# Seven half-size products in place of eight for the gate and up products of an FFN, on one Trainium2 core

## The reference, cut to what matters

```
h = layernorm(x)                       # 2048 x 512
W = scale * (4-bit weight - zero)      # 512 x (2 x 1376), unpacked on the chip
hidden = silu(h @ W_gate) * (h @ W_up) # 2048 x 1376
x = x + hidden @ W_down                # 1376 x 512
```

## Time and profile before

| | |
|---|---|
| median of 3 executions | 2420.39 us (2418.84 to 2422.48) |
| the profiled execution's own time | 2423.2 us |
| its span, first to last instruction | 2421.4 us |
| TensorE busy | 2368.5 us, 98% |
| granted TensorE clock, mean | 0.993 |
| FFN steps (1, 1) to (4, 3) | 1078.8 to 1321.5 us of the span |

### The profile page before, as it was taken

The page is one execution under the profiler, slowest core; times in us unless marked ns, Lnnn a source line. Parts: engine busy times, 40 slices in busy tenths (PEclk is TensorE's granted clock), DMA queues, the critical chain, the costliest instruction groups (busy, mean ns, idle before and its releaser), DMA issues.

```text
span 2421.4 us, 45108 instructions
## 1 busy us (share of the span) xinstructions
PE 2368.5 (98%) x17660; PEld 1297.3 (54%) x17668; DVE 1624.8 (67%) x3133; ACT 1252.7 (52%) x2423; POOL 1226.8 (51%) x983
## 2 busy tenths in 40 slices
PE   8899999999999999999999989999999999999998
PEld 4555555555555555444444655555555555555554
DVE  8877777777777798754444666667666666656566
ACT  7666565655555555333232554555555555544453
POOL 4556666666666666233232445445555555445531
PEclk9999999999999999999999999999999999999999
DMA  6111121212121111011100011122121212221101
GB/s 211 45 45 36 45 53 27 54 27 53 32 55 30 42 40 28 27 44 36 44 11 30 27 31 28 44 53 62 36 62 36 62 36 62 53 43 27 27 14 70
DMA packets 216753, 108.13 MB, mean 45 GB/s; under 512 B 169280, under 2 KB 192480, under 8 KB 216544
## 3 DMA queue, kind: packets, MB, share of 16 engines
q1 hardware_dynamic: 216544, 105.25, 17.6%
HBM read 61.62 MB, written 4.19 MB: 27 GB/s over the span
## 4 chain that ended last, share of the span: by engine, by line
PE 63%; POOL 14%; DVE 12%; ACT 5%; issue 5%; DMA 0%; POOLq 0%; SPq 0%; DVEq 0%; ACTq 0%
PE PB L867 17%; PE PB L819 15%; PE PB L979 9%; PE PB L803 6%; POOL AR L2720 5%; PE PB L996 5%; POOL AR L2725 4%; POOL PSP L2738 3%; DVE WB L1938 2%; DVE AR L2136 2%; PE PB L844 2%; PE PB L909 2%; PE PB L775 1%; POOL AR L2715 1%; ACT JUNK L1332 1%
## 5 line engine op out<-in xcount | busy, mean ns | idle before, releaser
L867 PE MATMUL PB<-WB,AR 128*128 128x512 f16 x3072 | 685.5, 380 | 1.5 <-DVE AR L2136 1.1
L819 PE MATMUL PB<-XTB,WB 128*128 128x512 f16 x3072 | 682.3, 381 | 2.6 <-DVE WB L1938 1.5
L867 PEld LDWEIGHTS PB<-WB,AR 128*128 128x128 f16 x3072 | 298.5, 98 | 356.7 <-issue 8.5
L819 PEld LDWEIGHTS PB<-XTB,WB 128*128 128x128 f16 x3072 | 298.3, 98 | 348.7 <-issue 10.3
L2731 POOL TENSOR_TENSOR AR<-AR,SML 128x512 f32<-128x512 f32 x128 | 144.7, 1152 | 317.1 <-DVE SML L2121 317.1
L2151 DVE SCALAR_TENSOR_TENSOR X<-PB,SML,X 128x512 f32<-128x512 f32 x256 | 189.3, 747 | 169.4 <-PE PB L867 163.4
L1492 ACT ACTIVATE AR<-PB 128x512 f16<-128x512 f32 x256 | 131.4, 595 | 232.6 <-PE PB L909 232.4
L2031 DVE TENSOR_TENSOR AR<-PB,AR 128x512 f16<-128x512 f32 x128 | 88.2, 691 | 168.0 <-ACT AR L1455 168.0
L2720 POOL TENSOR_TENSOR AR<-AR,CST 128x512 f32<-128x512 f32 x128 | 183.0, 1430 | 31.3 <-ACT AR L1402 31.3
L979 PE MATMUL PB<-XTB,AR 128*128 128x512 f16 (+1 forms) x864 | 192.5, 379 | 0.0
L1408 ACT ACTIVATE AR<-AR 128x512 f16<-128x512 f32 x128 | 80.5, 630 | 196.1 <-POOL AR L2725 194.7
(11 more groups left out here) (273 smaller groups left out, 3775.7 us busy)
## 6 DMA issues: line engine op xcount, KB each, us to landing
STG<-in_wo SPq DMA_DIRECT2D x14, 1024.0 KB
STG<-in_wq SPq DMA_DIRECT2D x13, 1024.0 KB
STG<-in_qw_gu SPq DMA_DIRECT2D x40, 128.0 KB
STG<-in_ctxT SPq DMA_DIRECT2D x4, 1024.0 KB
X<-in_x SPq DMA_DIRECT2D x4, 1024.0 KB, 10.8
out_x<-X SPq DMA_DIRECT2D x16, 256.0 KB, 2.4
STG<-in_wk SPq DMA_DIRECT2D x14, 256.0 KB
STG<-in_wv SPq DMA_DIRECT2D x14, 256.0 KB
```

What stands on the lines that cost most here:

```text
L819: m = pe.do.matmul(b[:, :], wq[x][:, k, h * 128:(h + 1) * 128], XT[y][c][:, k, :], start=n == 0, stop=n == 11)
L867: m = pe.do.matmul(b[:, :], AT[x][:, h, t * 128:(t + 1) * 128], wo[y][:, h, :], start=n == 0, stop=n == 11)
```

## The change

It applies to blocks s = 2, 3, 4, all chunks: twelve steps, called folded. W's block and x's chunk are seen as 2 by 2 blocks: K in two halves of 256, hidden columns in two tiles of 128 (gate and up side by side), tokens in two sets of 256. Eight block products become seven (P1 to P7), each two outputs (gate, up) of 2 slices of K x 3 = 6 matmuls 256 wide: 84 matmuls. P5, P6 and P7 multiply two sums of blocks, P3 and P4 one sum and one block, P1 and P2 two blocks.

- The sums of W (4 per block, `fold_w`, 512 columns each) are made on GpSimd, in the staging area, their halves on ScalarE and GpSimd (`fold_w_halves`). The staging area is free for the next load only after that.
- The sums of x (per chunk 4 `join_x` and 4 `fold_x` on GpSimd; 4 `fold_x_halves`, each one ScalarE copy and one VectorE subtraction; 512 columns each). They go where the context halves `CTB` lie, which the second layer needs: so `CTB` (4 x 1 MB) is written to DRAM after unit 12 of the first attention, and read back behind step (4, c).
- P1 is copied out of PSUM by ScalarE, VectorE adds the others to buffers in SBUF (`CB`): 7 additions per step. Silu, hidden values and their halves then work in 4 pieces of 256 tokens rather than 2 of 512.
- In the planner: unpacking of block 2 moves to (1,0) side 3, (1,1) sides 0, 1 and 3; the down weights of block s + 1, s from 1 to 4, to (s,3) sides 0 and 2 (only side 0 for s = 4). The places of `unpack` during blocks 2 to 4 stay.

```diff
+            def product(s, c, name, b, wt, xs):
+                for g in range(2):
+                    n = 0
+                    o = b[:, 256 * g:256 * g + 256].rearrange("p (a n) -> p a n", a=2)
+                    for k in range(2):
+                        for x, y in THREE:
+                            m = pe.do.matmul(o, wt[x][:, k, g, :], xs[y][:, k, :, :], start=n == 0, stop=n == 5)
+                            n += 1
+                m.then_inc(gu_mm.of((s, c, name)), 1)
...
+                product(s, c, "P1", bank(0, (p_out, (s, c, "P1"))), a11, b11)
...
+                product(s, c, "P6", bank(1, (p_sum, (s, c, "P1+P6"))), sw[1], sx[1])
+                product(s, c, "P5", bank(2, (p_sum, (s, c, "P1+P6+P5")), (p_sum, (s, c, 1, 1))), sw[0], sx[0])
+                product(s, c, "P2", bank(3, (p_sum, (s, c, 0, 0))), a12, b21)
...
+                product(s, c, "P7", bank(1, (p_sum, (s, c, "P1+P6+P7"))), sw[2], sx[2])
+                product(s, c, "P3", bank(0, (p_sum, (s, c, 0, 1))), sw[3], b22)
+                product(s, c, "P4", bank(3, (p_sum, (s, c, 1, 0))), a22, sx[3])
...
                 side("f", s, c, 0)
-                gate_up(s, c, 0)
+                if folded(s, c):
+                    folded_first(s, c)
+                else:
+                    gate_up(s, c, 0)
                 side("f", s, c, 1)
                 down(*FFN[i - 1], (0, 1))
                 side("f", s, c, 2)
-                if s < 5:
+                if folded(s, c):
+                    folded_last(s, c)
+                elif s < 5:
                     gate_up(s, c, 1)
                 down(*FFN[i - 1], (2, 3))
                 side("f", s, c, 3)
```

ScalarE's order in a folded step:

```diff
+                    product_out(s, c, "P1", 0, (0, 0))
+                    folded_gate(s, c, 0, 0)
+                    folded_hidden(s, c, 0, 0)
+                    side("f", s, c, 1)
+                    side("f", s, c, 2)
+                    folded_gate(s, c, 1, 1)
+                    folded_gate(s, c, 0, 1)
+                    folded_hidden(s, c, 1, 1)
+                    folded_gate(s, c, 1, 0)
+                    folded_hidden(s, c, 0, 1)
+                    folded_hidden(s, c, 1, 0)
+                    side("f", s, c, 3)
```

VectorE's part, in the places where `hidden` stood, and the sums of x:

```diff
+            def fold_x_halves(c, i):
+                dve.wait_ge(xs_hi, (c, i))
+                dve.do.tensor_tensor(SUMX[1][c][i], XF[i], SUMX[0][c][i], ALU.subtract).then_inc(xs_lo.of((c, i)), 1)
+
+            def product_add(s, c, key, name, bank, dst, src):
+                dve.wait_ge(gu_mm, (s, c, name))
+                dve.do.tensor_tensor(CB[BLOCK[dst]], PB[bank][:, :], CB[BLOCK[src]], ALU.add).then_inc(p_sum.of((s, c, *key)), 1)
...
+            def folded_first(s, c):
+                dve.wait_ge(p_out, (s, c, "P1"))
+                product_add(s, c, ("P1+P6",), "P6", 1, (1, 0), (0, 0))
+                dve.wait_ge(p_sum, (s, c, "P1+P6"))
+                product_add(s, c, ("P1+P6+P5",), "P5", 2, (0, 1), (1, 0))
+                product_add(s, c, (0, 0), "P2", 3, (0, 0), (0, 0))
+                folded_hidden(s, c, 0, 0)
+
+            def folded_last(s, c):
+                product_add(s, c, ("P1+P6+P7",), "P7", 1, (1, 0), (1, 0))
+                dve.wait_ge(p_sum, (s, c, "P1+P6+P7"))
+                product_add(s, c, (1, 1), "P5", 2, (1, 1), (1, 0))
+                product_add(s, c, (0, 1), "P3", 0, (0, 1), (0, 1))
+                folded_hidden(s, c, 1, 1)
+                product_add(s, c, (1, 0), "P4", 3, (1, 0), (1, 0))
+                folded_hidden(s, c, 0, 1)
+                folded_hidden(s, c, 1, 0)
```

The planner and SyncE:

```diff
-                where = (((2, 3), (3, 0), (3, 1), (3, 2)), ((0, 3), (1, 1), (1, 3), (2, 1)))[s][k] if s < 2 else \
+                where = (((2, 3), (3, 0), (3, 1), (3, 2)), ((0, 3), (1, 0), (1, 1), (1, 3)))[s][k] if s < 2 else \
                     (k // 2, 1 + 2 * (k % 2))
...
-                plan_f(*(((0, 3, 3), (1, 0, 1))[j] if s == 0 else (s, 2, 2 + j if s == 1 else 1 + 2 * j)), "unpack_d", s + 1, j)
+                plan_f(*(((0, 3, 3), (1, 0, 1))[j] if s == 0 else (s, 3, 2 * j)), "unpack_d", s + 1, j)
+
+        for step, places in ((2, ((1, 2, 0), (1, 2, 1), (1, 2, 2), (1, 2, 3))), (3, ((2, 2, 0), (2, 2, 1), (2, 2, 2), (2, 2, 3))),
+                             (4, ((3, 2, 0), (3, 2, 1), (3, 2, 2), (3, 2, 3)))):
+            for n, where in enumerate(places):
+                for i in ((0, 2), (1, 3))[n % 2]:
+                    plan_f(*where, "fold_w_halves" if n > 1 else "fold_w", step, i)
+        for c, places in ((0, ((0, 2, 1), (0, 2, 2), (0, 2, 3), (0, 3, 0), (0, 3, 1), (0, 3, 2))),
+                          (1, ((0, 3, 3), (1, 0, 0), (1, 0, 1), (1, 0, 2), (1, 0, 3), (1, 1, 0))),
+                          (2, ((1, 3, 0), (1, 3, 1), (1, 3, 2), (1, 3, 3), (2, 0, 0), (2, 0, 1))),
+                          (3, ((2, 0, 2), (2, 0, 3), (2, 1, 0), (2, 1, 1), (2, 1, 2), (2, 1, 3)))):
+            for n, where in enumerate(places):
+                for i in ((0, 1), (2, 3), (0, 2), (1, 3), (0, 1), (2, 3))[n]:
+                    plan_f(*where, ("join_x", "fold_x", "fold_x_halves")[n // 2], c, i)
...
-                return [(uq_lo, (key[1], KT - 1))]
+                return [(ws_lo, (key[1], 3)) if 2 <= key[1] <= 4 else (uq_lo, (key[1], KT - 1))]
...
+                sp.do.dma_start(kept[:, 4096 * c:4096 * c + 4096], CTB[:, 4096 * c:4096 * c + 4096]
...
+                    if (L, u) == (0, 12):
+                        keep_contexts()
```

More of the change, by code:

```diff
@@ L94, in build @@
         every = []
+        kept = nc.dram_tensor("kept", (128, 4096 * NC), F16, kind="Internal").ap()
         def signal(name):
@@ new lines, in folded_last @@
+            def folded_last(s, c):
+                pl = place(s)
+                a22 = [w_part(GUW[pl][n], 1, 1) for n in range(2)]
+                b22 = [x_part(n, c, 1, 1) for n in range(2)]
+                sw = [[SUMW[pl][n][i].rearrange("p (k g n) -> p k g n", k=2, g=2) for n in range(2)] for i in range(4)]
+                sx = [[by_kan(SUMX[n][c][i]) for n in range(2)] for i in range(4)]
+                product(s, c, "P7", bank(1, (p_sum, (s, c, "P1+P6+P7"))), sw[2], sx[2])
+                product(s, c, "P3", bank(0, (p_sum, (s, c, 0, 1))), sw[3], b22)
+                product(s, c, "P4", bank(3, (p_sum, (s, c, 1, 0))), a22, sx[3])
@@ L1355, in high @@
                     act.wait_ge(y_mm, (0, 3, 3))
+                    if kind == 2:
+                        act.wait_ge(xs_lo, (3, 3))
                 elif (L, g) == (1, 1):
@@ L1558, in gated @@
                 if i > 0 and j < len(step_tiles(FFN[i - 1][0])):
-                    act.wait_ge(h_lo, (*FFN[i - 1], j))
+                    for key in h_keys(*FFN[i - 1], j):
+                        act.wait_ge(h_lo, key)
                 if i == 0:
@@ L1576, in hidden, with fold_w_halves, product_out, folded_gate @@
                 act.do.activation(HB[(4 * s + c) % 2][0][0:wd, j, :], SG[j][0:wd, :], copy).then_inc(h_hi.of((s, c, j)), 1)
+            def fold_w_halves(s, i):
+                j, ki = SUM_AT[i]
+                act.wait_ge(wf, (s, i))
+                act.do.activation(SUMW[place(s)][0][i].rearrange("p (k g n) -> p k g n", k=2, g=2),
+                                  w_part(AREA[0].rearrange("p (k f) -> p k f", k=4), ki, j), copy).then_inc(ws_hi.of((s, i)), 1)
+            def fold_x_halves(c, i):
+                act.wait_ge(ct_kept[c], c)
+                act.wait_ge(v_mm, (0, UNIT[0][NKV - 1, c], 0))
+                act.wait_ge(xf, (c, i))
+                act.do.activation(SUMX[0][c][i], XF[i], copy).then_inc(xs_hi.of((c, i)), 1)
+            def product_out(s, c, name, bank, block):
+                before_it = FFN[FFN.index((s, c)) - 1]
+                act.wait_ge(gu_mm, (s, c, name))
+                if folded(*before_it):
+                    act.wait_ge(hf, (*before_it, *block))
+                act.do.activation(CB[BLOCK[block]], PB[bank][:, :], copy).then_inc(p_out.of((s, c, name)), 1)
+            def folded_gate(s, c, j, t):
+                act.wait_ge(p_sum, (s, c, j, t))
+                for key in h_keys(*FFN[FFN.index((s, c)) - 1], j):
+                    if len(key) == 3 or key[3] == t:
+                        act.wait_ge(h_lo, key)
+                act.do.activation(sg_part(j, t), CB[BLOCK[j, t]][:, 0:256], ACTF.Silu, scale=power(("sc", 0))).then_inc(silu_ok.of((s, c, j, t)), 1)
+            def folded_hidden(s, c, j, t):
+                i = FFN.index((s, c))
+                act.wait_ge(hf, (s, c, j, t))
+                act.wait_ge(y_mm, (*FFN[i - 2], 3))
+                act.do.activation(hb_part(s, c, 0, j, t), sg_part(j, t).rearrange("p (a n) -> p a n", a=2), copy
+                                  ).then_inc(h_hi.of((s, c, j, t)), 1)
             def tail_setup(part):
@@ L2655, in vector @@
                 side("f", s, c, 0)
-                hidden(s, c, 0)
+                if folded(s, c):
+                    folded_first(s, c)
+                else:
+                    hidden(s, c, 0)
```

(9 more changed lines are left out.)

124 lines of the change are left out of this document (113 added, 11 removed).

## The result

The changed kernel takes 2427.76 us (median of 8 runs, 2425.11 to 2430.93) against 2421.01 for the kernel before (8 runs, 2418.84 to 2422.54): ratio 1.003, 95% interval 1.002 to 1.0039, 6.75 us more. The forecast was 2417.5. The profiled execution took 2428.07, its span is 2425.1.

What follows compares the result with a forecast made beforehand. TensorE was taken to bound the FFN. Products -14.4, waits +2.4, +7.1, +0.5 and +1.5 sum to -2.9 us: profiled execution 2420.3, median 2417.5 us, range 2409 to 2428.

Steps and rivals of the forecast that it cites:

- The products: Folded steps on TensorE: 84 matmuls at 0.109 us, 9.17 instead of 10.37 us a step, 14.4 us less in twelve.
- Wait 1: (1,1) side 0: TensorE waits 2.4 us, uncovered, for VectorE's multiply from bank 5, shared by two adjacent unpackings.
- Wait 2: (2,0) to (2,2): VectorE, late with x sums and unpacking, frees banks late; 3.8 + 0.2 + 1.6 + 1.5, 7.1 us.
- Wait 3: (3,3) into (4,0): ScalarE's 5.0 us scaling delays the silus, so the down product waits 0.5 us for a hidden half.
- Wait 4: (4,3) side 2: the late load of w(1,1,1) delays ScalarE's squares, so the `peak` matmul waits 1.5 us.
- The DMA's zero: Context write after unit 12 and reads back in (4,1) to (5,0): taken to cost 0 us.
- B: Rival: VectorE bounds every step with unpacking, its instructions stretched beside GpSimd; +7 us, 2427.5; chance 0.25.
- A: Rival: waits mostly absorbed, lateness in (1,3) and (2,0) partly parallel; -10 us, 2410.4; chance 0.28.
- C: Rival: products miss the 0.109 us pace, at 0.13 a step's take 10.9 us; +14 us, 2434; chance 0.05.

Runs made afterwards that it cites:

- unpacking_moved_only: The kernel before with only the unpacking of slices 1, 2 and 3 in block 1 moved to (1,1) sides 0, 1 and 3; ratio 1.0008.
- contexts_only: The kernel before with only the write of the context halves to DRAM and the reads back; 2420.41 us, ratio 0.9999.
- last_sums_later: The changed kernel with the four halvings of chunk 3's x sums moved from (2,1) sides 2 and 3 to (2,2) sides 0 and 1; 2428.33 us.

## Why the prediction was wrong

The products were right: 1.31 us per product, 1.20 per step (block 3 is 4.8 us shorter, four steps), 14.4 in all. By the prediction's estimate from the section Back-to-back issue gap of TensorE: Matmul & The Clock Gate in the Trainium skill the new kernel was to lose 23 us here; the trace disagrees, at 256 wide as at 512 (0.109 and 0.216 us a matmul).

What failed is the step that sized and listed the waits, 11.5 us on record, 18.0 and 3.75 of clock in the trace. It put the clock at nothing without a reason, took VectorE's shifts and hidden pieces as if nothing of GpSimd's stood beside them, and left out two waits:

- **Wait 1**: 2.4 on record, 3.23 measured. The working holds without the sums (2.45 in the run unpacking_moved_only); I took the earlier trace rows's 0.48 for the shift although GpSimd now had its differences to make at that very moment. 1.26 it was.
- **Wait 2**: 3.8 + 0.2 + 1.6 + 1.5 on record, 4.97 + 0 + 2.35 + 2.21 measured. The chain is the one on record, almost to its times: with P1 at 1132.13, ScalarE has copied P1 6.55 us later (6.6 on record), VectorE has added P2 at 9.2 (9.0). Then the hidden piece took 1.03 and the shift 1.37 where I had 0.48 and 0.48, both beside GpSimd's `low` (lines below), and the addition that frees bank 6 was over at 17.3 instead of 15.8. The three places that showed were right; the fourth, 0.2 in (2,1), did not show.
- **Wait 3**: 0.5 on record, 1.23 measured, for GpSimd's low half in (4,0), as named. **Wait 4**: 1.5 on record, 1.11 measured, for ScalarE's squares.
- **Not on record**: 2.02 us in (2,3). `unpack_d`'s matmul wants bank 4, which `peak` holds until VectorE has come to its reduction, behind the additions; I walked the banks for the moved unpacking of the gate/up weights, not for the moved down weights. Also 0.86 in (1,0), VectorE late there by chunk 0's halvings.
- **Not on record**: the clock, 3.75 us. I priced a wait by its own length only.

VectorE's and GpSimd's timelines of the changed kernel behind wait 2's chain (L2436 a hidden piece, L2396 a shift, L2428 the subtractions for sums of x, L2463 the additions to x, L2900 `low`):

```profile
1141.93 1.03 DVE L2436 SCALAR_TENSOR_TENSOR AR<-AR,SML,PSP 128x256 f32<-128x256 f32 x1 [0.58 <-ACT AR L1724]
1142.88 1.37 DVE L2396 TENSOR_SCALAR STG<-STG,SHC 128x512 uint32<-128x512 uint32 x1
...
1146.91 1.83 DVE L2428 TENSOR_TENSOR CTB<-WB,CTB 128x512 f16<-128x512 f32 x2 [1.22 <-ACT CTB L1710]
1148.67 1.40 DVE L2463 SCALAR_TENSOR_TENSOR X<-PB,SML,X 128x512 f32<-128x512 f32 x2
```

```profile
1138.84 5.13 POOL L2900 TENSOR_TENSOR WB<-AR,WB 128x512 f16<-128x512 f32 x4
```

Together 3.6 us by size, 2.9 by waits not seen, 3.75 by the clock: 10.2, which takes -2.9 to +7.3. The DMA's zero was right (contexts_only); the write itself is 10.2 us at 410 GB/s, not 10.5, on which nothing hangs. Wait 1 had no cover, as written.

Of the rivals, B gave 2427.5, the number that came, and its instructions (a shift of over 1.2 us, hidden pieces of 1.0) are what stretched the chain. That the number fits is luck. With B's own figures, 0.9 for two shifts and 1.0 for four hidden pieces, the demand is 14.7 + 0.8 + 2.1 = 17.6 us, not 16.6, and B would have come out about 4 us higher. And its mechanism is not the one that was shown: it had all steps with unpacking over their time, with waits in (3,1) and (4,1). Block 3 has none. The overload is in (2,0) to (2,2) alone, where the sums of x stand in VectorE's order on top of two unpackings a step; there it is real, as last_sums_later showed. A, waits absorbed, and C, the pace, fell.

The Trainium skill's line on contention (GPSIMD Engine Reference, specification table: SBUF interfaces shared with VectorE) was used in the prediction to price rival B and not the forecast's own steps. The line speaks of VectorE instructions in a 2-port perf mode or with two SBUF inputs; the trace agrees for the halvings and the hidden pieces, which have two. The shift, with one tensor from SBUF, stretches here as well (1.26, 1.37); whether it runs in such a mode, no run here shows. `product_add`, with one input from PSUM, takes 0.67 to 0.69 us in all 84 instances, whatever GpSimd does. Rows by line: least/median/most ns, first and last start:

```profile
L2428 DVE TENSOR_TENSOR CTB<-WB,CTB x16: 677/1216/1743, 1053.7 to 1180.0; 128x512 f16<-128x512 f32 x16
L2432 DVE TENSOR_TENSOR PSP<-PB,PSP x48: 673/683/693, 1139.4 to 1325.6; 128x512 f32<-128x512 f32 x48
L2436 DVE SCALAR_TENSOR_TENSOR AR<-AR,SML,PSP x24: 471/484/1373, 1141.9 to 1326.9; 128x256 f32<-128x256 f32 x24
```

## What to carry to other kernels

A fold that saves matmuls pays only what is left after its side work, and that side work is paid where it gathers: list, for each bank and each engine's order, the last user ahead of every moved piece, and take an instruction's duration beside whatever the change itself sets next to it (in these traces, VectorE's shifts, hidden pieces and subtractions pay the rest of the GpSimd instruction that they start beside). When a wait is removed and the time hardly moves, add up the waits of the new trace before trying the next edit: here only taking work out of the crowded steps, not shifting it within them, turned +6.75 us into -8 to -9.
